# A down projection split over two column halves of TensorE's array, with one tile's tokens on each half

## What is computed

```python
def first(x, kind):                      # x: [128, 64, 256]
    nr  = gelu(x @ w1_nr  + b1_nr)  @ w2_nr  + b2_nr
    tsr = gelu(x @ w1_tsr + b1_tsr) @ w2_tsr + b2_tsr
    h   = gelu(x @ w1_sr  + b1_sr)                       # 512 wide
    sr  = gelu(h @ w2_sr + b2_sr) @ w3_sr + b3_sr
    out = where(kind == 0, nr, where(kind == 1, tsr, where(kind == 2, sr, 0)))
    return layer_norm(x + out) * gamma + beta

def second(y, domain):
    hidden = gelu(y @ down_W.T + down_b)                 # 256 -> 64, the down projection
    hidden = hidden @ expert_W[domain].T + expert_b[domain] + domain_emb[domain]
    return layer_norm(hidden @ up_W.T + up_b + y) * ln_gamma + ln_beta
```

## Time and profile before

| | us |
|---|---|
| median of 3 runs | 286.7 |
| the profiled execution, its own time | 286.11 |
| the span that its trace covers | 284.3 |
| PE busy | 266.5 |
| PEld busy | 255.1 |
| ACT busy | 203.7 |
| DVE busy | 197.0 |
| POOL busy | 150.0 |
| records of L1065, 132 matmul passes, busy | 34.1 |

### The profile page before, as it was taken

How to read it: one execution, slowest core, us unless ns; L and a number is a source line. 1 busy time by engine, 2 the same in 40 slices (tenths; PEclk the granted TensorE clock), 3 DMA queues, 4 the chain that set the end, 5 groups by cost and what they waited for, 6 DMA issues and landing times.

```text
span 284.3 us, 8145 instructions
## 1 busy us (share of the span) xinstructions
PE 266.5 (94%) x2051; PEld 255.1 (90%) x2052; DVE 197.0 (69%) x669; ACT 203.7 (72%) x451; POOL 150.0 (53%) x166
## 2 busy tenths in 40 slices
PE   8599999999999999899999999999999999999860
PEld 7388989999999998799999999999999999998760
DVE  7676633426646745688788888878888887878772
ACT  3357687867777775678887878887887888787510
POOL 3212634734756747445556654665664556565444
PEclk9869999999999999999999999999999999999995
DMA  6462110110221121132332424233243423331122
GB/s 201 115 236 45 40 38 2 40 42 1 58 66 37 47 74 36 38 82 68 90 80 67 102 78 113 68 83 83 65 105 80 110 68 79 87 80 55 53 64 76
DMA packets 44028, 20.98 MB, mean 74 GB/s; under 512 B 37783, under 2 KB 42182, under 8 KB 44008
## 3 DMA queue, kind: packets, MB, share of 16 engines
q1 hardware_dynamic: 41508, 15.28, 21.9%
q0 software_dynamic: 1584, 4.33, 4.7%
q10 hardware_dynamic: 916, 1.13, 1.4%
HBM read 12.02 MB, written 8.65 MB: 73 GB/s over the span
## 4 chain that ended last, share of the span: by engine, by line
PE 85%; DVE 5%; issue 3%; ACT 3%; ACTq 2%; POOLq 0%; POOL 0%; DVEq 0%
PE ps_h L933 21%; PE ps_z L1010 11%; PE ps_u L1056 10%; PE ps_d L1065 10%; PE ps_z L1015 5%; PE ps_t L1027 5%; PE ps_z L968 5%; PE ps_u L968 5%; PE ps_z L998 3%; PE ps_t L1117 3%; PE ps_t L1114 3%; PE ps_t L1115 3%; PE ps_u L902 2%; DVE st L647 1%; ACT zn L805 1%
## 5 line engine op out<-in xcount | busy, mean ns | idle before, releaser
L443 POOL TENSOR_TENSOR h_lo<-h,h_hi 128x256 fp32r<-128x256 f32 (+1 forms) x75 | 69.8, 931 | 95.7 <-ACT h L798 95.7
L798 ACT ACTIVATE h_hi<-ps_h,per_feature_sb 128x256 fp32r<-128x256 f32 x84 | 38.2, 479 | 23.2 <-PE ps_h L933 23.1
L448 POOL TENSOR_TENSOR rs<-ve,minus_half 128x4 f32<-128x4 f32 x36 | 40.9, 1137 | 24.5 <-DVE ve L636 24.4
L624 DVE BATCH_NORM_STATS2 st<-ps_z 128x6 f32<-128x256 f32 x66 | 24.8, 415 | 33.1 <-PE ps_z L1015 33.1
L805 ACT ACTIVATE zn<-ps_z,nm,rs 128x256 f32<-128x256 f32 x66 | 33.7, 562 | 9.3 <-DVE nm L640 8.7
L458 POOL DMA_INDIRECT out<-o,out_rows_now x33 | 34.9, 1059 | 6.2 <-issue 6.2
L798 ACT ACTIVATE h<-ps_h,per_feature_sb 128x256 f32<-128x256 f32 x84 | 38.0, 481 | 0.0
L821 ACT ACTIVATE yt<-ps_t,per_feature_sb 128x256 f32<-128x256 f32 x66 | 34.0, 573 | 5.2 <-PE ps_t L1027 5.2
L1056 PE MATMUL ps_u<-table_hi,stack 128*128 x132 | 35.9, 302 | 0.0
L604 DVE TENSOR_TENSOR x_lo<-x,x_hi 128x512 fp32r<-128x512 f32 x33 | 23.5, 712 | 17.8 <-ACT x_hi L780 17.8
L1065 PE MATMUL ps_d<-yt,per_feature_sb 128*128 128x256 f32 x132 | 34.1, 380 | 1.4 <-ACT yt L821 1.3
(11 more groups left out here) (153 smaller groups left out, 696.9 us busy)
## 6 DMA issues: line engine op xcount, KB each, us to landing
x<-in_x_feat SPq DMA_DIRECT2D x130, 64.0 KB
out<-o SPq DMA_DIRECT2D x66, 64.0 KB, 2.0
last_sb<-in_last_w SPq DMA_DIRECT2D x1, 768.0 KB, 5.1
out<-o,out_rows_now POOLq DMA_INDIRECT x33, 2.6
w_sr_sb<-in_w_sr SPq DMA_DIRECT2D x1, 512.0 KB, 3.7
w_sr_sb<-in_w_sr ACTq DMA_DIRECT2D x1, 512.0 KB, 5.0
w_two_sb<-in_w_two SPq DMA_DIRECT2D x1, 512.0 KB, 5.7
per_unit_sb<-in_per_unit ACTq DMA_DIRECT2D x1, 325.0 KB
```

Of the source, the lines that this page charges most:

```text
L443: pool.tensor_tensor(dst, full, high.bitcast(F32), ALU.subtract).then_inc(ready, 1)
L448: pool.tensor_tensor(RS[p][:, :, :], VE[p][:, :, :], mhalf[:, :].rearrange("p (n t) -> p n t", n=2), ALU.pow).then_inc(rstd, 1)
L798: ins = act.activation(dst[:, m, :], src[m], ACT.Gelu, bias=COL[:, bass.ds(col + m, 1)])
```

## The change

Four things change, and no instruction moves past another.

- `DD` holds the down weight once, 64 columns instead of 128, and the input `per_feature` is narrower by 128 columns (64 KB less to load).
- `down` issues four instructions instead of two: for each chunk c and each tile t, 64 columns of weights by the 128 tokens of tile t, into rows 64 t to 64 t + 63 of `DP[:, 0:128]`. The built program gives them the tile size 128 x 64, at column 0 for t = 0 and at column 64 for t = 1. The outputs are made once, not twice: tile 0's lie on rows 0 to 63 and tile 1's on rows 64 to 127.
- `adapter_gelu` issues three activations instead of two: for each tile 64 rows by 128 columns into its own rows of the stack, and one of 128 rows by 128 columns in full fp32 into `GF`.
- `stack_low` issues four operations instead of two, each on 64 rows by 128 columns. Each tile's low part goes to the other 64 rows than its high part: to rows 64 to 127 for tile 0, to rows 0 to 63 for tile 1. `X2` is filled from each tile's own rows.

```diff
-        GF = [sb(f"gelu_f{p}", [P, N]) for p in range(2)]
+        GF = [sb(f"gelu_f{p}", [P, P]) for p in range(2)]
...
             def stack_low(slot, q):
 
                 dve.wait_ge(g_act, slot + 1)
-                lo = pair_cols(S[q])[A:P]
-                dve.tensor_tensor(lo, GF[q][A:P, :].rearrange("p (a b t) -> p a b t", a=TT, b=2),
-                                  lo.bitcast(F32), ALU.subtract)
-                dve.tensor_copy(pair_cols(X2[q])[0:A], pair_cols(S[q])[0:A].bitcast(F32)).then_inc(s_made, 1)
+                for t in range(TT):
+                    own, other = slice(t * A, t * A + A), slice(A - t * A, P - t * A)
+                    dve.tensor_tensor(two_cols(S[q], t)[other], two_tokens(GF[q][own, :]),
+                                      two_cols(S[q], t)[own].bitcast(F32), ALU.subtract)
+                for t in range(TT):
+                    own = slice(t * A, t * A + A)
+                    ins = dve.tensor_copy(two_cols(X2[q], t)[0:A], two_cols(S[q], t)[own].bitcast(F32))
+                ins.then_inc(s_made, 1)
...
             def adapter_gelu(slot, q):
 
                 act.wait_ge(d_ps, slot + 1)
-                src = DP[:, 0:N].rearrange("p (a b t) -> p a b t", a=TT, b=2)
-                act.activation(pair_cols(S[q]), src, ACT.Gelu, bias=COL[:, COL_DOWN_B:COL_DOWN_B + 1])
-                act.activation(GF[q][A:P, :], DP[A:P, 0:N], ACT.Gelu,
-                               bias=COL[A:P, COL_DOWN_B:COL_DOWN_B + 1]).then_inc(g_act, 1)
+                for t in range(TT):
+                    own = slice(t * A, t * A + A)
+                    act.activation(two_cols(S[q], t)[own], two_tokens(DP[own, 0:P]), ACT.Gelu,
+                                   bias=COL[own, COL_DOWN_B:COL_DOWN_B + 1])
+                act.activation(GF[q][:, :], DP[:, 0:P], ACT.Gelu,
+                               bias=COL[:, COL_DOWN_B:COL_DOWN_B + 1]).then_inc(g_act, 1)
...
                 pe.wait_ge(yt_act, slot + 1)
                 for c in range(KC):
-                    ins = pe.matmul(DP[:, 0:N], DD[:, c, :], YT[q][:, c, :], start=(c == 0), stop=(c == KC - 1))
+                    for t in range(TT):
+                        ins = pe.matmul(DP[t * A:t * A + A, 0:P], DD[:, c, :], YT[q][:, c, t * P:t * P + P],
+                                        start=(c == 0), stop=(c == KC - 1))
                 ins.then_inc(d_ps, 1)
...
-            np.concatenate([down, down], axis=2).reshape(P, -1),
+            down.reshape(P, -1),
```

More of the change, by code:

```diff
@@ L76, in conditioned_layers @@
         WL = {n: sb(n + "_lo", [P, c + LW * (n == "last")], F32R) for n, c in W_COLS.items()}
-        FEAT = sb("per_feature_sb", [P, COLS + KC * 2 * A + 2 * H])
+        FEAT = sb("per_feature_sb", [P, COLS + KC * A + 2 * H])
         COL = FEAT[:, 0:COLS]
-        DD = FEAT[:, COLS:COLS + KC * 2 * A].rearrange("p (c m) -> p c m", c=KC)
-        G2 = FEAT[:, COLS + KC * 2 * A:].rearrange("p (v n) -> p v n", v=2)
+        DD = FEAT[:, COLS:COLS + KC * A].rearrange("p (c m) -> p c m", c=KC)
+        G2 = FEAT[:, COLS + KC * A:].rearrange("p (v n) -> p v n", v=2)
         UNIT = sb("per_unit_sb", [A + 1, H + 2 * E + TE * 2 * A])
@@ L241, in conditioned_layers @@
         EARLY_UNIT = H + 2 * E + 2 * TABLE_BANKS * 2 * A
-        EARLY_FEAT = COLS + KC * 2 * A
+        EARLY_FEAT = COLS + KC * A
         PAIRS_IN_STEP = {-1: (3, 4), 0: (5, 6), 1: (7, 8)}
@@ L314, in kind_of, with two_cols, two_tokens @@
             return values(eng, IDS[0:1, 1, bass.ds(slot * G, 1)], OTHER)[0]
-        def pair_cols(tile):
-            return tile[:, :, 0:3:2, :]
+        def two_cols(tile, t):
+            return tile[:, t, 0:3:2, :]
+        def two_tokens(ap):
+            return ap.rearrange("p (b t) -> p b t", b=2)
         def flat(ap):
```

## The result

The changed kernel takes 283.66 us (median of 4 runs, 283.57 to 283.76) beside 287.02 us for the kernel before (4 runs, 286.64 to 287.73). The ratio is 0.989, with a 95% interval of 0.986 to 0.992: faster by 1.1%, or 3.4 us. The forecast was 287.4, no change with a lean to slower; the time lies at the low end of its range, where the rival "the halves share every window" had put 284.1. Beside the experiments the kernel before has medians of 286.35, 286.32 and 286.60 us (19, 17 and 14 runs), lower than 287.02; so the gain is as likely near the 2.4 us by which the profiled spans differ (284.3 and 281.9) as at 3.4.

A forecast was written before the change was run, and what follows sets the result against it. TensorE, never stopping in later steps, was taken as the bound. Five windows and two shape changes add 0.025 us a slot, 0.8 over 32; the end -0.05; 0.7 on 286.7 gives 287.4 us, range 283.5 to 292.5.

The forecast's parts named there:

- the halves share every window: Down projection: four windows, passes of both column halves always together; -0.08 us a slot, -2.6 us, 284.1 us; chance 0.17.
- The windows: Down projection: eight passes in program order take five windows of 0.1075 us, 0.54 us in place of 0.86.
- The price of the shapes: Around the down projection: next load 0.20 us after the last pass, then in the open; 0.145 us in, 0.20 out.
- Halves that never work together: Down projection: eight windows, no sharing; +0.35 us a slot, +11.2 us, 297.9 us; chance 0.15.
- Loads in the open within the down projection: Each window grows by up to 0.055 us; up to +7.8 us, middle +3.9, 290.6 us; chance 0.12.
- Every load waiting for the pass ahead: Down projection: nothing overlaps, eight passes of 0.1075 + 0.055 us; +0.73 a slot, +23 us, 310 us; chance 0.02.
- VectorE as the bound: VectorE's four operations overrun its 0.70 us of room; +7 us, likelier about +2, 289 us; chance 0.05.
- Cost 0: Each slot: ScalarE's added 0.06 us and VectorE's added 0.27 us are covered by waits, adding nothing.
- The end: Last slot: down projection shorter by 0.32 + 0.055 us, gelu longer by 0.06, stack by 0.27; sum -0.05 us.
- The likeliest case: Down projection in five windows; 0.025 us more a slot, 287.4 us in total; chance 0.49.

The follow-up runs named there:

- the runs with half a tile: Changed kernel with tile 1's products on 64 of their 128 tokens, chunks outside, then tiles outside: 284.07 and 286.56 us, one run each.
- two independent pairs of kernels: Both tiles on one half against the earlier kernel's full-array cut: 295.94, 285.84 us; changed kernel, small full-array product between chunks against ahead: 297.7, 287.74 us.

## Why the prediction was wrong

**The windows.** The step that failed is "passes start in the order of the program ... only the second of one tile can share a window with the first of the next". Measured: four windows in place of five, with pairs 7 ns apart, and the runs with half a tile show the younger tile's passes overtaking. The rows that I leaned on could not show this, since in none of them do neighbours use different halves. A pass that never had a reason to overtake says nothing about whether it may. The term of the sum was 4 x 0.1075 = 0.43 us from the first window's start to the fifth's; measured are 3 x 0.109 = 0.33 to the fourth's, and the 0.05 of open load beside it. That made a slot 0.025 us longer on paper, and 0.08 shorter in the trace.

**The price of the shapes** held. Load 0.20 us after the last pass going in (153.59 to 153.79) and coming out (154.19 to 154.38), and 10 to 11 us for all of it in two independent pairs of kernels, beside 11. The rival's sum, 1.21 - 0.08 a slot, is what the trace has: 1.13. But the reading behind the price was not complete: the same trace of the kernel before has changes of shape behind the longer passes of L902 (fp32, 256 columns), where the next load starts 0.30 us after the last pass, as from 28.45 to 28.76. The price of 0.20 belongs to short passes, and that the new ones are short made it fit.

**The total.** With four windows the sum gave -2.6 us, on the spans it is -2.4, on the medians -3.4 with an interval from 2.3 to 3.9. So the size of the rival was right. By stages the traces have 1.86 us in the 24 later steps (24 x 0.08 = 1.9) and 0.33 in the eight steps before them: six "sr" steps, 10.45 before and 10.34 to 10.41 now, win 0.45, the first wins nothing, and the one at the change of kinds loses 0.13. Another 0.34 lie ahead of the first step, and the part behind the last step's start loses 0.13. The 0.34 can't be put down to the change: the first step begins anywhere from 28.2 to 30.5 us in the traces of these experiments.

**The other rivals.** Halves that never work together, eight windows: there are four. Loads in the open within the down projection: once, 0.05 us behind the first pass, and that was in the sum. Every load waiting for the pass ahead: the loads start 2 ns after a pass has begun, on halves and on the full array. VectorE as the bound: TensorE is busy in all 6.08 us of a later step, as it was in all 6.14.

**ScalarE and VectorE.** Groups by shape of the changed kernel, to be read beside the earlier trace rows:

```profile
L822 ACT ACTIVATE stack<-ps_d,per_feature_sb 64x128 fp32r<-64x128 f32 x66 | 23.9, 363 | 4.3 <-PE ps_d L1076 2.6 <-issue 0.8
...
L698 DVE TENSOR_TENSOR stack<-gelu_f,stack 64x128 fp32r<-64x128 f32 x66 | 19.3, 293 | 3.9 <-ACT gelu_f L824 2.6
...
L702 DVE CAST stack_hi<-stack 64x128 fp32r<-64x128 f32 x66 | 14.6, 221 | 0.9
```

A subtraction is 0.293 us (0.29 forecast), a copy 0.221 (0.21), an activation 0.363, and 0.368 for the third (0.34): together 0.10 more than forecast. In the repeated steps all of it is covered. "Cost 0" is right there only: at the change of kinds and in DRAIN the cover is not there, and about 1 us goes, of which the sum had 0.33, in the last slot. The wait before L608 was to fall from 0.70 to 0.4; it is 0.15 in one step and absent in the next, as the step is shorter too. VectorE is now busy 5.49 of 6.08 us:

```profile
153.79:159.87 6.08, 6.08 (x54) 5.76 (x53) 5.49 (x21) 5.00 (x13) 3.50 (x5) 1.00 0.35 86
```

**The end** was forecast at -0.05 and is -0.04 from the last down projection on (14.37 to 14.33): the part from its start to the gelu falls from 1.17 to 0.71 us, and gelu and stack take back the rest. What it left out is the slot before, where TensorE's wait for `zn` grows from 0.15 to 0.63 us; the stretch from the last bias product to the last down projection is 0.17 us longer, and not shorter.

**The chances.** The likeliest case got 0.49 on an argument from order, and four windows 0.17. No row spoke for either; with the two cases weighted alike, the forecast would have been between them. That a fall of the clock at the change of kinds can add 1.6 us to an execution was in no case of mine.

## What to carry to other kernels

Products that use different column halves of the array ran side by side in both orders tried, as long as no half had more than four passes on its list; eight passes in a row for one half left the other empty for the first four. At each change between the full array and halves 0.20 us go by from the start of the last pass to the next load, where 0.11 would go by without a change, and then the first load is in the open. In and out together cost 0.30 to 0.35 us, so a short block of halves between full-array products must win more than that, and two such blocks put together would pay it once (not tried). The full gain of the halves was 0.43 us a slot, and 0.08 of it were left. Where the program itself stands still, a shorter product only makes the hole larger, and may cost the clock. And work that is covered in the repeated steps can still show where the pipeline runs out.

## What the runs showed of the hardware that was not expected

- The second half's first pass starts 7 ns after the first half's when two passes stand ahead of it in the program, 13 to 14 ns when four do: about 3.4 ns a pass with its load.
- The depth of a half's list: one running and three waiting passes, in two kernels.
- A change of shape lets the next load start 0.20 us after the start of a last pass of up to 0.11 us, and 0.30 after one of 0.215 (L902 in the kernel before); after passes of 16 columns it is 0.19.
- fp32r passes of 256 columns stand 0.113 or 0.118 us apart, depending on what ran ahead of them. In a step of kind "sr" of the kernel before the second group of twelve takes 1.41 us, and 1.36 with the down projection cut in four on the full array, other work being equal; with the passes around it the step is 10.33 us in place of 10.45. That kernel is 0.25% faster than before (0.9975, 0.9955 to 0.9996) for this reason as far as the trace shows. What decides between the two spacings is open. The chain of the kernel before, and then that of the kernel with the cut:

```profile
66.28 1.41 PE ps_h L933 x12
```

```profile
56.12 1.36 PE ps_h L933 x12
```
